# Three 16-head cross attentions: the softmax's scores are computed twice, the second time with keys on the partitions, in place of 384 transposes per call

## The reference, cut to what matters

```python
q, k, v = heads(xn @ Wq + bq), heads(ctx @ Wk + bk), heads(ctx @ Wv + bv)   # 16 heads of width 16
# layer 0 only: q and k are rotated by position, and keys with mask == 0 get a score of -1e30
scores = einsum('bqhd,bkhd->bhqk', q, k) / 4          # 100 queries x 361 keys for each batch and head
attn = softmax(scores, axis=-1)                       # layer 1 only: attn * gate[key]
x = x + einsum('bhqk,bkhd->bqhd', attn, v) @ Wo + bo
```

## Time and profile before

| | us |
|---|---|
| median of 3 runs (2272.12 to 2282.67) | 2280.46 |
| the profiled execution, its own time | 2281.18 |
| its span, first to last instruction | 2279.2 |
| `l0x`: start 225.6, last add ends 508.5 | 282.9 |
| `l1x`: start 746.5, last add ends 951.6 | 205.1 |
| `l3x`: start 1976.4, last add ends 2181.0 | 204.6 |

### The profile page before, as it was taken

The page is one execution under the profiler, slowest core; times in us unless marked ns, Lnnn a source line. Parts: engine busy times, 40 slices in busy tenths (PEclk is TensorE's granted clock), DMA queues, the critical chain, the costliest instruction groups (busy, mean ns, idle before and its releaser), DMA issues. The chain is left out here.

```text
span 2279.2 us, 30680 instructions
## 1 busy us (share of the span) xinstructions
PE 1711.9 (75%) x10556; PEld 1224.0 (54%) x10556; DVE 1069.9 (47%) x2341; ACT 728.8 (32%) x1482; POOL 331.8 (15%) x247
## 2 busy tenths in 40 slices
PE   4998688779789799879996177728925572199978
PEld 4887455546478566568885055517712220066643
DVE  2544465655543457520000623320028899736665
ACT  1222135543288256422221122212213300026630
POOL 0000100000021101031112100020022994101000
PEclk9999798988855899889998578958968775599989
DMA  3000100001000000143653100044120000100010
GB/s 142 1 0 6 46 1 1 1 9 35 26 1 0 25 1 2 63 146 114 209 190 111 43 22 14 7 176 149 55 68 0 0 0 0 73 0 2 2 45 15
DMA packets 41358, 102.73 MB, mean 45 GB/s; under 512 B 9789, under 2 KB 27690, under 8 KB 36404
## 3 DMA queue, kind: packets, MB, share of 16 engines
q1 hardware_dynamic: 29194, 56.85, 7.2%
q0 software_dynamic: 7216, 39.63, 5.2%
q10 hardware_dynamic: 4830, 4.71, 0.7%
HBM read 89.28 MB, written 11.88 MB: 44 GB/s over the span
## 5 line engine op out<-in xcount | busy, mean ns | idle before, releaser
L2602 PE MATMUL wide<-l3a_qk,ident 100*100 100x512 f32 x144 | 80.3, 714 | 51.1 <-POOL l3a_qk L2692 50.3
L2030 PE MATMUL summed<-l1f_pack,l1f_hidden 128*100 128x256 f32 x480 | 107.3, 382 | 2.9 <-ACT l1f_hidden L2079 2.9
L2164 DVE TENSOR_TENSOR l1f_out<-summed,l1f_b 100x512 f32<-100x512 f32 x15 | 10.4, 692 | 187.8 <-PE summed L2030 187.8
L2030 PEld LDWEIGHTS summed<-l1f_pack,l1f_hidden 128*100 128x100 f32 x480 | 78.9, 167 | 27.9 <-ACT l1f_hidden L2079 5.9
L1209 ACT ACTIVATE l0x_pr<-l0x_sc,l0x_nmx 100x361 f32<-100x361 f32 x128 | 75.1, 593 | 56.8 <-DVEq L1352 55.9
L1350 DVE CUSTOM_DVE_ANT_0 l0x_sc<-wide,l0x_words 100x361 f32<-100x361 f32 x128 | 68.4, 534 | 50.6 <-PE wide L1068 33.2
L2079 ACT ACTIVATE l1f_hidden<-wide,l1f_pack 128x200 f32<-128x200 f32 x120 | 48.9, 426 | 135.0 <-PE wide L2024 82.8
L1078 PE MATMUL turned<-ident,l0x_pr 100*121 100x100 f32 x384 | 62.8, 305 | 35.5 <-DVE l0x_pt L1340 22.3
L2692 POOL TENSOR_TENSOR l3a_qk<-l3a_cw,l3a_score 100x1024 f32<-100x1024 f32 x36 | 86.6, 2438 | 4.3 <-DVE l3a_score L2756 4.3
L1078 PEld LDWEIGHTS turned<-ident,l0x_pr 100*121 100x121 f32 x384 | 52.0, 208 | 63.9 <-ACT l0x_pr L1209 42.3
L2024 PE MATMUL wide<-l1f_rt,l1f_pack 128*128 128x200 f32 x480 | 83.9, 333 | 0.7 <-ACT l1f_rt L2089 0.7
(11 more groups left out here) (523 smaller groups left out, 3931.6 us busy)
## 6 DMA issues: line engine op xcount, KB each, us to landing
l2f_w<-l2f_w_dram SPq DMA_DIRECT2D x16, 1024.0 KB
ctxt<-ctxt_dram SPq DMA_DIRECT2D x4, 1083.0 KB, 8.1
l1f_sorted_x<-l1f_zeros SPq DMA_DIRECT2D x15, 200.0 KB
l1f_rows<-l1f_sorted_x SPq DMA_DIRECT2D x15, 200.0 KB
l1f_sorted_y<-l1f_out ACTq DMA_DIRECT2D x15, 200.0 KB
l2x_ctxt<-ctxt_dram SPq DMA_DIRECT2D x8, 361.0 KB
l0f_w<-l0f_w_dram SPq DMA_DIRECT2D x18, 128.0 KB
l1f_shared<-l1f_shared_dram SPq DMA_DIRECT2D x1, 2052.0 KB
```

Source lines behind the costliest of these rows:

```text
L2030: last = pe.matmul(banks[0:S, c, 0:E], hidden[:, f, c * S:(c + 1) * S], w2_of(w, f), start=f == 0, stop=f == FC - 1)
L2164: dve.tensor_tensor(out[:, slot], summed[0:S, :, 0:E], b2[:, slot, :].unsqueeze(1).broadcast_to([S, RT, E]), ALU.add).then_inc(sem["y_read ...
L2602: last = pe.matmul(wide[0:S, 2 * (t % 2) + half, :], net.ident[0:S, 0:S], ring[:, n % RING, half * HALF:(half + 1) * HALF], start=u == 0, ...
```

## The change

- **Layout.** `kt` becomes `[P, B, NQ, PADKV]`: each head of a quad has a strip of 32 partitions, holding one row of -1, the 16 dimensions of the key, in `l0x` a row with the mask (0 or -2^100), and the rest unused. `q4` has the same strips for the queries: row 0 of a strip is 0 (later the maximum), then the 16 dimensions, and in `l0x` a row of 1 for the mask. A product over 17 (18) rows is then score - maximum (+ mask) at once. `headmask`, `qm` and GpSimd's masked copies go, and so does the reordering of weight columns.
- **Spreading.** Engines write keys and queries in the old layout (`kd`, a ring of four batches, and `qt`), and SyncE moves them to the strips by DMA: per call 64 DMAs for keys (16 partitions x 2 x 361), 16 for queries, and in `l0x` 16 for the mask. ScalarE (in `l0x` VectorE) waits for a spread before it writes over the ring, and for all spreads before its first exp. GpSimd first fills `kt` with -1, the pads and `mx` with 0, and `q4` with 0 (in `l0x` by a copy of `maskone`).
- **Loop.** Scores with queries on the partitions (L1112, two heads at a time) serve only for the maxima (`highest`, L1401). TensorE turns the maxima (L1117), VectorE adds them to a copy of the quad's queries (`with_maxima`, L1414, to `q2`), and TensorE computes the scores again, keys on the partitions, three chunks of 121 keys a head (`score_by_key`, L1127). ScalarE's exp (L1266) reads them and writes `pt` itself. The transposes of `pr`, `pr` itself and the copies to `pt` are gone. `TURN` makes the two heads of `score_by_key` lie in strips other than those of the two scores ahead of them.
- **Tails.** All eight follow the loop, double buffered. In `l0x` the mask is in the product, and VectorE makes the mask's row and a factor `some` per batch ahead of the values.
- **Loads.** TensorE waits for `wk` alone, then for `wv` ahead of the first values, then for the rest.

```diff
-    SLOT_HEAD = [...]
+    R, ROWS, TURN, KRING = 32, 1 + D + (1 if key_mask else 0), (2, 3, 0, 1), 4
...
+                def spread_keys(pair):
+                    sp.wait_ge(sem["k_ready"], 2 * KC * (pair + 1))
+                    for j in range(P // D):
+                        to = R * (j % Q) + 1
+                        for b in (2 * pair, 2 * pair + 1):
+                            sp.dma_start(kt[to:to + D, b, j // Q::2, 0:SKV], kd[j * D:(j + 1) * D, b % KRING, :, :]).then_inc(kt_spread[pair], 16)
...
+                spread_keys(0)
+                for half in range(2):
+                    spread_queries(half)
+                for pair in range(1, B // 2):
+                    spread_keys(pair)
...
-                        m, t, j = slot_of(g, i)
-                        pe.matmul(wide[0:S, i, 0:SKV], qm[64 * t:64 * t + 64, b % 2, m, j, :], kt[64 * t:64 * t + 64, b, m, :],
+                    for i in (2 * pair, 2 * pair + 1):
+                        pe.matmul(wide[0:S, i, 0:SKV], q4[R * i:R * i + ROWS, g, b, :], kt[R * i:R * i + ROWS, b, g, 0:SKV],
...
-                def turn(n, heads):
-                        for c in range(NCH):
-                            last = pe.transpose(turned[0:CH, i % 2, c * S:(c + 1) * S], pr[:, h % 8, c * CH:(c + 1) * CH], net.ident[0:S, 0:S])
+                def turn_maxima(n):
+                    pe.wait_ge(sem["m_ready"], 2 * n + 2)
+                    pe.transpose(wide[:, 2, LOW:LOW + S], mx[:, n % 2, :], net.ident[0:S, 0:S]).then_inc(sem["mt_psum"], 1)
+
+                def score_by_key(n, turns):
+                    b, g = n // NQ, n % NQ
+                    pe.wait_ge(sem["q2_ready"], n + 1)
+                    for j in turns:
+                        h, i = Q * n + j, TURN[j]
+                        if h >= 3:
+                            pe.wait_ge(sem["p_ready"], h - 2)
+                        for c in range(NCH):
+                            last = pe.matmul(scored[h % 3][0:CH, c * S:(c + 1) * S], kt[R * i:R * i + ROWS, b, g, c * CH:(c + 1) * CH],
+                                             q2[R * i:R * i + ROWS, n % 2, :], start=True, stop=True)
+                        last.then_inc(t_psum[j % 2], 1)
...
                 for n in range(QUADS + 2):
+                    if n + 1 < QUADS:
+                        score(n + 1, 0)
                     if 1 <= n <= QUADS:
-                        turn(n - 1, (0, 1))
+                        score_by_key(n - 1, (0, 1))
                     if n < QUADS:
-                        score(n)
+                        turn_maxima(n)
+                    if n + 1 < QUADS:
+                        score(n + 1, 1)
                     if 1 <= n <= QUADS:
-                        turn(n - 1, (2, 3))
+                        score_by_key(n - 1, (2, 3))
-                    (back, turn_y or project_y of the batch before)
                     if n >= 2:
                         weigh(n - 2)
+                for b in range(B + 2):
+                    if b < B:
+                        back(b)
+                    if 1 <= b <= B:
+                        turn_y(b - 1)
+                    if b >= 2:
+                        project_y(b - 2)
...
-                        act.activation(pr[:, h % 8, 0:SKV], src, ACT.Exp, bias=nmx[:, n % 2, i:i + 1], scale=-1.0).then_inc(sem["p_ready"], 1)
+                        act.activation(pt[:, h % 8], scored[h % 3][0:CH, 0:NCH * S].rearrange("s (c t) -> s c t", c=NCH), ACT.Exp).then_inc(sem["p_ready"], 1)
...
+                for spread in kt_spread:
+                    act.wait_ge(spread, 2 * SPREAD)
+                for spread in q_spread:
+                    act.wait_ge(spread, SPREAD)
...
+                pool.memset(kt[:, :, :, 0:SKV], -1.0)
...
+                    dve.tensor_tensor(q2[:, n % 2, :], q4[:, g, b, :], wide[:, 2, LOW:LOW + S], ALU.add).then_inc(sem["q2_ready"], 1)
```

More of the change, by code:

```diff
@@ L930, in cross_attn16 @@
     SCALE = D ** -0.5
+    R = 32
+    ROWS = 1 + D + (1 if key_mask else 0)
+    MASKED = -2.0 ** 100
+    TURN = (2, 3, 0, 1)
+    KRING = 4
+    LOW = 400
     HALF = B // 2
@@ L1174, in keys @@
                         act.wait_ge(sem["k_ready"], KC * (b - 2) + m + 1)
+                    if not rope and b >= KRING:
+                        act.wait_ge(kt_spread[(b - KRING) // 2], 2 * SPREAD)
                     if biases:
@@ L1219, in copy_yt @@
[L1219 to L1234 removed]
+                    act.wait_ge(sem["yt_psum"], b + 1)
@@ new lines, in copy_yt @@
+                    if b >= 2:
+                        act.wait_ge(sem["out_psum"], b - 1)
+                    act.activation(yt[:, b % 2], wide[:, 2 + b % 2, 0:KC * S].rearrange("p (k s) -> p k s", k=KC), ACT.Copy).then_inc(sem["yt_ready"], 1)
+                for spread in kt_spread:
+                    act.wait_ge(spread, 2 * SPREAD)
+                for spread in q_spread:
+                    act.wait_ge(spread, SPREAD)
+                for n in range(QUADS):
+                    exps(n, range(Q))
+                    if n % NQ == 0 and n >= NQ:
+                        take(n // NQ - 1)
@@ L1311, in rotated_queries @@
                     dve.drain()
-                    dve.tensor_tensor(dst, dst, qsin[:, m, :].rearrange("p (b s) -> p b s", b=HALF), ALU.add).then_inc(sem["q_ready"], 1)
+                    if not key_mask:
+                        dve.tensor_tensor(dst, dst, qsin[:, m, :].rearrange("p (b s) -> p b s", b=HALF), ALU.add).then_inc(sem["q_ready"], 1)
+                    else:
+                        dve.tensor_tensor(dst, dst, qsin[:, m, :].rearrange("p (b s) -> p b s", b=HALF), ALU.add)
+                        dve.drain()
+                        dve.tensor_tensor(dst, dst, some[:, half * HALF:(half + 1) * HALF].unsqueeze(2).broadcast_to([P, HALF, S]), ALU.mult).then_inc(sem["q_ready"], 1)
                 for b in range(B):
@@ new lines, in _ @@
+                for n in range(QUADS + 1):
+                    if n < QUADS:
+                        highest(n, 0)
+                    if n >= 1:
+                        with_maxima(n - 1)
+                    if n < QUADS:
+                        highest(n, 1)
+                for b in range(B + 2):
+                    if b < B:
+                        invert(b)
+                    if b >= 2 and bo is not None:
+                        add_bias(b - 2)
+                    dve.drain()
+                    if b < B:
```

333 lines of the change are left out of this document (160 added, 173 removed).

## The result

The changed kernel is slower: 2429.08 us (median of 4 runs, 2426.07 to 2430.86) against 2280.39 for the kernel before beside it, a ratio of 1.0652 (95% interval 1.0623 to 1.0681). Forecast were 2189 and a range up to 2265. The span grew from 2279.2 to 2429.1 us, and nearly all of it lies in the three calls: `l0x` takes 290.9 us (282.9 before), `l1x` 272.3 (205.1) and `l3x` 269.9 (204.6), 140 of the 150 us.

A forecast was written before the change was run, and what follows sets the result against it. TensorE was taken to bound `l1x` and `l3x`, the round trip TensorE, VectorE, ScalarE, TensorE to bound `l0x`. Gains 59.6 + 17.6 + 14.6 = 92 off 2281.2 gave 2189 us, range 2105 to 2265.

The forecast's parts named there:

- The clock: TensorE in the new loop: granted clock stays at 1.00, as the old loop's rows show with transposes half the time.
- The quad: TensorE per quad in the loop: two halves of 1.23, maxima's transpose 0.28, weighing 0.70, together 3.45 us.
- All strips free: Rival for the loop: second head doesn't wait for the first, 2.60 us a quad, total 2110; chance 0.13.
- Where the loop starts: Setup before the loop: first exp at 322.4 in `l0x`, 807.5 in `l1x` (810.8 before), 2039.9 in `l3x`.
- I cost the ring at nothing: Setup: ScalarE's ring of keys doesn't wait for spreads, cost nothing, with a margin of 1 to 2 us.
- All projections move 5.9 earlier: Setup of `l1x`: TensorE waits only for `wk` and `bk`, some 749.7 instead of 755.60, so projections start 5.9 earlier.
- The transfers' landing: Setup, after the last 16 spreads are issued: landing taken as 2 us, between nothing and 8.1.
- GpSimd's fill ... 9.8: Setup: GpSimd fills 11,552 columns in 9.8 us, done at 757, ahead of the first spread.
- Tails: All eight batches' tails after the loop: 1.6 per batch, some 3 to fill and empty, 16 us; ends 12.8 and 24.
- The sum: First exp to end of a call: 2.0 first quad, 107.0 for 31 quads, 1.5 to last weighing, 16 tails: 126.5.
- The rival with the clock: Rival for the loop: granted clock stays at 1.2 GHz, some 6.2 us a quad, total 2440; chance 0.03.
- The break-even of 4.44 us a quad: Loop: 3.45 + 92 / 93 = 4.44 us a quad, from which the rival without strip overlap (2352, chance 0.10) decides.

The follow-up runs named there:

- full32: Changed kernel with 32 full matmuls (128 rows, 128 columns of weights, 100 moving columns) added per quad behind the maxima's transpose; 2880.82 us, ratio 1.264.
- the queue's edits: Changed kernel redone with 64 rows per matmul, plus merged spreads, the last pair's issued by two engines, and an early exp table load; 2196.97 us, ratio 0.9703.
- warm_start: Changed kernel with 64 full matmuls once ahead of each loop, behind the last spread's wait; 2490.88 us, ratio 1.093.
- old_tails_last: Kernel before the change, with only its eight tails moved behind the loop, one after another without overlap; 2377.96 us, ratio 1.048.

## Why the prediction was wrong, by its steps

**The clock: the step that failed.** The forecast took 1.00 for the new loop from the old loop's rows, "with transposes half of the time", and gave 0.03 to the other case. The old rows can't say that: they are of a list with 64 and 100 rows per matmul, and the change took just these out. The new loop has 0.50 in all three calls; the same list with 32 full matmuls a quad has 1.00, with 32 narrow ones 0.50. The cost of it, an estimate, is (5.52 - 3.02) x 93 = 232 us, nearly all of the 240 between forecast and result; it takes 3.02, the quad of `full32` without a wait, for what the loop would have at 2.4 GHz. (The Trainium skill says that activity releases the throttle and calls it busy-ness, TensorE: Matmul & The Clock Gate, "Part 1: The HAM clock gate". A loop that is busy for 165.00 of 165.00 us at 0.50 shows that busy time, as the profile counts it, is not that activity.)

**The quad: mechanism half right, size off.** 3.45 us forecast, 3.02 measured at 2.4 GHz (`full32`). Matmuls do start beside those of other strips. The other half, that one doesn't start ahead of what stands before it in the list, isn't borne out: a head doesn't wait until the one ahead of it has only its last left, it starts 0.53 us behind it (901.29, 901.82; at 2.4 GHz 0.30, 1110.73 and 1111.03, where the forecast had four gaps, 0.42) and then they alternate. "All strips free", 2.60, goes too far. At the high clock 93 x 0.43 = 40 us more would have been gained than forecast, by the same estimate.

**Where the loop starts: wrong by 35 us.** Counted from the call's start, the first exp of `l0x` came 1.7 us later than forecast, that of `l1x` 19.1, of `l3x` 77.5 - 63.5 = 14.0. Two terms failed. One is "I cost the ring at nothing": an issue takes 0.59 with 0.66 from one to the next, not 0.45, and 80 of them fill the setup, so ScalarE's ring (7.6 us in `l1x`, 8.0 in `l3x`) and the first exp wait for the queue. Merging the spreads gave back 7.7 us in `l1x`, 10.1 in `l3x` and 5.0 in `l0x`. The other is "All projections move 5.9 earlier": TensorE's did start early, but VectorE's stall holds the gates, and with them ScalarE's first keys, so the first spread of `l1x` starts 24.3 us into the call (780.99 - 756.7) where the forecast's own times have 14.4 (766.8 - 5.9 - 746.5). As the queue then hardly pauses, up to 10 of the 19 us may come from there; that is an estimate from these rows, not a run. The transfers' landing, 2, was right (2.2 in the page). The exp table's load, 1.28, came behind the wait, where it is seen. "GpSimd's fill ... 9.8" was 9.73, but "done at 757, ahead of the first spread" was the wrong question: it stops VectorE. What the fill costs on the path is not measured: moving it only moved the stall; a kernel without it wasn't tried.

**Tails.** 16 forecast, 19.8 measured (from the last L1139, 1009.2, to 1029.0), within the 12.8 to 24 given: 11 us over three calls. A batch takes 2.29 us where 1.6 was forecast; VectorE stands idle for 0.85 of it, until TensorE's `project_y`.

**The sum.** From first exp to end a call takes 192.3 where 126.5 was forecast: 3 x 65.8 = 197. With the 35 of the setup that is 232; the last 8 lie outside the calls. The rival with the clock said 2440, from a quad of 6.2 that was too long (the whole doesn't quite double: 3.02 to 5.52) and a setup that was too short. Had the clock held, the total would be, by the same estimate, 2429 - 232 = 2197, close to the forecast, but by errors that cancel: strips better by 40, setup worse by 35, tails by 11. The break-even of 4.44 us a quad was the right test, and 5.52 fails it.

## What to carry to other kernels

When an edit swaps matmuls over many rows for matmuls over few, the clock of the old loop says nothing on the new one: price it at 1.2 GHz as a main case, or build the edit so that rows stay at work (here 64 at a time, which won 1.5%, and 3% with the queue's edits, where 17 lost 6.5%). Keep the row tiles of matmuls that should overlap at one size. Count a queue's issues at the price of one, 0.6 us, and set the sum against the whole stage, before a wait on it is put at nothing.

## What the runs showed of the hardware that was not expected

- TensorE, busy without a gap, is held at 1.2 GHz for a whole loop of 17-row matmuls (0.50 in 840:1005), also when it enters the loop at 2.4 GHz (0.50 from 881 in `warm_start`). Tails one after another are at 1.2 too (`old_tails_last`), overlapped ones at 2.4 (the changed kernel).
- At half the clock the changed quad takes 1.83 times as long, not twice (5.52 us, against 3.02 in `full32`).
- Two strips whose chains stand one behind the other in the list run interleaved, record by record (901.29 to 902.54 above).
- A GpSimd fill of 9.7 us holds a VectorE tensor-scalar between SBUF tiles for up to 8.7 us (0.18 alone), wherever it comes; a reduction beside it keeps its time (0.35). (The Trainium skill has the cause, Trainium Architecture — The Big Picture, "What this means for kernel authors": the port pair that VectorE and GpSimd share is an exclusive lock. The traces agree for the one and show that not every instruction needs it.)
- An issue of a spread, 16 partitions from SBUF to SBUF, takes 0.59 us on SyncE for 45 KB, and 0.60 for twice that.
